# Attention of a LayerNorm, attention and low-rank FFN layer on 8 cores: K of the later half as a stage of its own, the quadratic in two VectorE operations, the output copies on VectorE

## The reference

```python
def polymax(x):                       # in place of softmax; x_int=-100, y_int=1
    lin  = where(-100 <= x <= 0, -0.01 * x + 1, 0)
    poly = where(x > 0, x ** 2 + 1, 0)
    return (poly + lin) / 1000
def attn(x, W_attn, W_proj):          # 16 heads of 64
    q, k, v = split(x @ W_attn)
    att = einsum('bhid,bhjd->bhij', q, k) / 8
    att = where(causal, att, -inf)
    return einsum('bhij,bhjd->bhid', polymax(att), v) @ W_proj
x = x + attn(layernorm(x), W_attn, W_proj)           # x: (4, 4096, 1024) f32
x = x + ffn(layernorm(x), U1, V1, b1, U2, V2, b2)    # rank 256, 4096 wide, gelu
```

## Time and profile before

| | us |
|---|---|
| median of 3 runs | 2106.52 (2102.57 to 2109.41) |
| the profiled execution, its own time | 2104.88 |
| its span on core 0, the slowest | 2103.3 |
| spans of the other cores | 2085.1 to 2102.9 |
| granted clock of TensorE, mean, core 0 | 0.732 of full speed |
| attention half 0, from its first scores to its last copy | 512.0 to 1189.1 |
| from there to the first matmul of V of the later half | 1189.1 to 1246.1 |
| running sums and V of the later half | 1246.1 to 1357.5 |
| attention half 1 | 1357.5 to 1620.8 |

### The profile page before, as it was taken

One profiled execution on the slowest core, in us unless ns is written; L12 is line 12 of the kernel. 1 busy time (PEld: TensorE's weight loads), 2 busy tenths in 40 slices (PEclk: granted clock), 3 DMA queues, 4 the chain that ended last, 5 costly groups with the idle time before them and its releaser, 6 DMA issues.

```text
span 2103.3 us, 22645 instructions; the slowest of 8 cores (2085.1 to 2103.3 us)
## 1 busy us (share of the span) xinstructions
PE 1285.4 (61%) x6801; PEld 457.9 (22%) x6880; DVE 1232.6 (59%) x2043; ACT 786.0 (37%) x1202; POOL 0.2 (0%) x4
## 2 busy tenths in 40 slices
PE   3423286477776676767667427666775461367786
PEld 0001132243222222212112113322221130023332
DVE  4558433244677887888878513489997233344422
ACT  1200000001667776767667400167776000133333
POOL 0000000000000000000000000000000000000000
PEclk8755597799566677777877769955666685579988
DMA  5545201200000000000000220000000444001111
GB/s 164 160 128 191 80 22 59 80 1 11 21 8 18 16 6 16 8 16 6 16 18 6 76 89 1 1 1 1 1 1 21 156 136 128 0 0 41 40 40 41
DMA packets 53335, 96.08 MB, mean 46 GB/s; under 512 B 2529, under 2 KB 24290, under 8 KB 53218
## 3 DMA queue, kind: packets, MB, share of 16 engines
q1 hardware_dynamic: 46498, 84.14, 12.6%
q10 hardware_dynamic: 6720, 10.49, 1.6%
HBM read 82.04 MB, written 12.58 MB: 45 GB/s over the span
## 4 chain that ended last, share of the span: by engine, by line
PE 44%; DVE 24%; issue 13%; DMA 11%; ACT 5%; SPq 1%; DVEq 1%; ACTq 0%
DVE poolD L766 12%; PE ps L801 7%; DMA poolD<-W_attn 6%; PE ps L732 5%; PE ps L851 4%; PE ps L1132 3%; PE ps L940 3%; PE ps L633 3%; PE ps L1038 3%; PE ps L655 3%; PE ps L613 3%; PE ps L1152 3%; ACT poolD L753 3%; DMA poolD<-W_proj 2%; DVE poolC L498 1%
## 5 line engine op out<-in xcount | busy, mean ns | idle before, releaser
L753 ACT ACTIVATE poolD<-ps 128x1024 bf16<-128x1024 f32 (+3 forms) x640 | 561.1, 907 | 739.9 <-PE ps L732 620.6
L766 DVE SCALAR_TENSOR_TENSOR poolD<-poolD 128x1024 bf16<-128x1024 bf16 (+3 forms) x640 | 654.5, 1062 | 69.3 <-ACT poolD L753 35.7
L801 PE MATMUL ps<-poolD,poolA 128*64 128x512 bf16 (+3 forms) x1280 | 299.2, 455 | 223.8 <-DVE poolD L766 114.9
L732 PE MATMUL ps<-poolB,poolA 64*128 64x512 bf16 (+3 forms) x1280 | 275.1, 456 | 56.5 <-ACT poolD L753 26.0
L801 PEld LDWEIGHTS ps<-poolD,poolA 128*64 128x64 bf16 x1280 | 89.1, 117 | 405.4 <-issue 403.7
L1144 ACT ACTIVATE poolC<-ps,sb_b1s 128x512 bf16<-128x512 f32 x128 | 87.6, 687 | 114.8 <-PE ps L1132 71.6
L758 ACT ACTIVATE poolD<-ps,consts 128x256 bf16<-128x256 f32 x256 | 124.3, 486 | 0.0
L732 PEld LDWEIGHTS ps<-poolB,poolA 64*128 64x128 bf16 x1280 | 64.4, 101 | 242.1 <-issue 241.7
L851 PE MATMUL ps<-poolC,poolD 128*128 128x512 bf16 x224 | 106.5, 476 | 0.0
L940 PE MATMUL ps<-poolD,poolC 128*128 128x512 bf16 x241 | 59.5, 393 | 58.8 <-DVE poolD L912 57.9
L809 PE MATMUL ps<-poolD,poolA 128*64 128x128 bf16 x512 | 83.0, 297 | 0.0
(11 more groups left out here) (100 smaller groups left out, 1135.2 us busy)
## 6 DMA issues: line engine op xcount, KB each, us to landing
poolD<-x_t SPq DMA_DIRECT2D x8, 2048.0 KB, 9.2
poolA<-x_t SPq DMA_DIRECT2D x8, 2048.0 KB, 9.6
poolD<-W_attn SPq DMA_DIRECT2D x12, 1024.0 KB, 4.9
poolD<-W_attn SPq DMA_DIRECT2D x16, 512.0 KB, 3.9
poolC<-x_own_t SPq DMA_DIRECT2D x8, 1024.0 KB, 5.8
y<-poolC SPq DMA_DIRECT2D x4, 2048.0 KB, 6.9
kf2scratch<-poolD SPq DMA_DIRECT2D x32, 128.0 KB, 1.7
poolA<-kf2scratch SPq DMA_DIRECT2D x4, 1024.0 KB, 15.6
```

The costliest lines, as they stand in the source:

```text
L732: e.matmul(o, l, r, skip_group_check=True, start=True, stop=True, tile_position=tp),
L753: e.activation(o, i, AF.Relu), inc="S")
L766: e.scalar_tensor_tensor(o, i, 0.01, i, ALU.add, ALU.mult),
L801: e.matmul(o, l, r, skip_group_check=True, start=st, stop=True, tile_position=tp),
```

## The change

Three things change. (1) With `K_ILV = False` all of the interleaved K work is gone from half 0: the 256 matmuls L851, the 32 copies L862 and their DMAs, the eight weight loads with L713, and the four DMAs that read the buffer back. In its place `p4_sweep(D, is_v=False)`, code that was there unused, runs between half 0 and the V sweep: it loads W of K in 8 pieces of 512 KB with their conversions, and then runs 32 groups of 8 matmuls of 512 columns, each copied by VectorE straight into kf; the 8 loads for V come after. (2) (r + 0.01) r is done as an addition of a constant into a new buffer ab2 (two slots) and then a product; the product waits for the addition, and the addition for the product two steps before. (3) The copies of the output at the end of a block are done by VectorE in half 0 too.

```diff
+        ab2 = [view(poolD, 14336, BF16, [128, 2, 512]),
+               view(poolD, 16384, BF16, [128, 2, 512])]
...
-            if half == 0:
+            if K_ILV and half == 0:
                 b.wait("sync", "T", p1_done["T"])
...
-                    if half == 0 and tb2 == 0:
+                    if K_ILV and half == 0 and tb2 == 0:
                         b.wait("sync", "V", kcast[hc - 1] if hc > 0 else p1_done["V"])
                         kdd = b.dma(kstage4[:, :, :],
...
                         b.wait("vector", "S", s_rel[sb])
+                        if idx >= 2:
+                            b.wait("vector", "V", gcnt[idx - 2])
+                        acnt = b.op("vector",
+                                    lambda e, o=ab2[idx % 2][:, :, 0:N],
+                                    i=eb[:, 2 * sb:2 * sb + 2, 0:N]:
+                                    e.tensor_scalar_add(o, i, 0.01), inc="V")
                         b.wait("vector", "T", g_rel[sb])
+                        b.wait("vector", "V", acnt)
                         gcnt[idx] = b.op("vector",
                                          lambda e, o=gb[:, 2 * sb:2 * sb + 2, 0:N],
+                                         a=ab2[idx % 2][:, :, 0:N],
                                          i=eb[:, 2 * sb:2 * sb + 2, 0:N]:
-                                         e.scalar_tensor_tensor(o, i, 0.01, i,
-                                                                ALU.add, ALU.mult),
-                                         inc="V")
+                                         e.tensor_mul(o, a, i), inc="V")
...
-                        if half == 0 and idx < 8:
+                        if K_ILV and half == 0 and idx < 8:
                             b.wait("tensor", "V", kcast[hc])
...
-                    if half == 0:
-                        b.wait("scalar", "T", tf_av)
-                    if half == 0:
+                    b.wait("vector", "T", tfence())
+                    if K_ILV and half == 0:
                         if ke_dma[kblk[0] % 2]:
...
-                        if half == 0:
-                            if chunk_final and j > 1:
-                                b.op("scalar", lambda e, o=dst, s=src,
-                                     pv=prefsnap[:, j, p:p + 1]:
-                                     e.activation(o, s, AF.Identity, bias=pv), inc="S")
-                            else:
-                                b.op("scalar", lambda e, o=dst, s=src:
-                                     e.mul(o, s, 1.0), inc="S")
-                        elif not chunk_final:
+                        if not chunk_final:
                             b.op("vector", lambda e, o=dst, s=src: e.tensor_copy(o, s),
                                  inc="V")
+                        elif c <= 1:
+                            if j == 1:
+                                b.op("vector", lambda e, o=dst, s=src: e.tensor_copy(o, s),
+                                     inc="V")
+                            else:
+                                b.op("vector", lambda e, o=dst, s=src,
+                                     pv=prefsnap[:, j, p:p + 1]:
+                                     e.tensor_scalar(o, s, pv, None, ALU.add), inc="V")
...
-        b.wait("sync", ke_dma[0], 16)
-        b.wait("sync", ke_dma[1], 16)
-        for i in range(4):
-            kfload.append(b.dma(kf[:, :, 512 * i:512 * (i + 1)],
-                                kf2_d[:, :, 512 * i:512 * (i + 1)]))
-        b.wait("vector", ke_dma[0], 16)
-        b.wait("vector", ke_dma[1], 16)
+        if K_ILV:
+            ...
+        else:
+            p4_sweep(D, is_v=False)
         p4_sweep(2 * D, is_v=True)
```

More of the change, by code:

```diff
@@ L231, in build_program @@
         abh = view(poolD, 13824, BF16, [128, 2, 128])
+        K_ILV = False
         kstage4 = view(poolD, 20480, F32, [128, 8, 128])
@@ L526, in emit_sweep_kt @@
                 b.wait("tensor", "V", sweep_state["snapV"])
-                if half == 1:
+                if K_ILV and half == 1:
                     b.wait("tensor", kfload[ktloc // 4], 16)
@@ L853, in emit_attention @@
                     av_done = b.cnt["T"]
-                    tf_av = tfence()
-                    b.wait("vector", "T", tf_av)
-                    if half == 0:
-                        b.wait("scalar", "T", tf_av)
-                    if half == 0:
+                    b.wait("vector", "T", tfence())
+                    if K_ILV and half == 0:
                         if ke_dma[kblk[0] % 2]:
@@ L950, in build_program @@
         b.wait_all("vector", h0_done, sems=("T", "S"))
-        b.wait("sync", ke_dma[0], 16)
-        b.wait("sync", ke_dma[1], 16)
-        for i in range(4):
-            kfload.append(b.dma(kf[:, :, 512 * i:512 * (i + 1)],
-                                kf2_d[:, :, 512 * i:512 * (i + 1)]))
-        b.wait("vector", ke_dma[0], 16)
-        b.wait("vector", ke_dma[1], 16)
+        if K_ILV:
+            b.wait("sync", ke_dma[0], 16)
+            b.wait("sync", ke_dma[1], 16)
+            for i in range(4):
+                kfload.append(b.dma(kf[:, :, 512 * i:512 * (i + 1)],
+                                    kf2_d[:, :, 512 * i:512 * (i + 1)]))
+            b.wait("vector", ke_dma[0], 16)
+            b.wait("vector", ke_dma[1], 16)
+        else:
+            p4_sweep(D, is_v=False)
         p4_sweep(2 * D, is_v=True)
```

## The result

The changed kernel takes 2131.6 us against 2108.4 before (medians of 8 runs each); the ratio is 1.0118, with a 95% interval of 1.0102 to 1.0134. It is slower by 1.2%, outside the range of 2068 to 2122 around the 2085 us of the forecast. In some executions one die shows a lower granted clock and takes longer; medians here are over all runs, ratios and their intervals leave those executions out.

The account below looks back on a forecast made before the run. VectorE bounds half 1; in half 0 K's TensorE work and weight DMA waits add to it. Half 0 -94.1, stretch to V +72.5, half 1 +1.4: -20.2 us on 2104.88, so 2085 us, range 2068 to 2122.

Parts of the forecast that it names:

- part 2: (r + 0.01) r as addition (0.424 us) and product (0.69 us), dependent gap 0.04 us; was to bring 11 us.
- the first rival: Dependent wait between addition and product costs 0.11 us instead of 0.04: +36 us, 2121 us; chance 8%.
- part 1: K moved from half 0 into its own stage: half 0 82.5 us less, stretch to first V matmul 72.5 more.
- the third rival: K nearly free in half 0, its own stage dearer; low clock stays, loads slower: 2100 to 2107 us; chance 10%.
- second rival: The addition runs at twice, not four times, the rate: 2222 us; chance 5%.
- Part 3: Half 0's output copies on VectorE cost nothing, covered by its wait for scores and relu; 36 us if uncovered.

Follow-up runs that it names:

- E2: Changed kernel with the product's wait for the addition attached to the product instead of an instruction of its own; 2091.8 us, ratio 0.9927.
- E13: Kernel before, with all waits directly ahead of a VectorE or ScalarE operation attached to it; 2082.6 us, ratio 0.9855.
- E15: Changed kernel, with all waits directly ahead of a VectorE or ScalarE operation attached to it; 2064.8 us, ratio 0.9772.
- E1: Changed kernel with (r + 0.01) r as one operation again, K stage and copies on VectorE kept; 2107.4 us, ratio 1.0003.
- E11: Kernel before, K still inside half 0, with the two operations and the product's wait attached; 2093.3 us, ratio 0.9929.
- E6: Changed kernel with the output copies of half 0 on ScalarE again; 2144.5 us, ratio 1.0150.
- E4: Changed kernel with the product taking r twice, so it does not wait for the addition (0.01 r left out of the result); 2031.2 us, ratio 0.9643.
- E3: Changed kernel with the next step's addition queued ahead of the product, three slots of ab2; 2163.6 us, ratio 1.0270.
- E8: E3 with two staging buffers in the three weight loads, first two V pieces fetched during K's matmuls; 2114.7 us, ratio 1.0004.

## Why the prediction was wrong

**The step that failed** is in part 2: "the dependent pair L451, L452 starts 0.72 us apart with a duration of 0.68, so duration + 0.04". The row was read rightly and stood for another thing: L452 carries its wait, while the product's is an instruction of its own in the queue. The code showed this, `ss=True` at L452 and `b.wait` in the diff. In the changed kernel the gap is 0.10 us, the value at which the prediction said that it would fall. That is the first rival, which had a chance of 8% and a price of 36 us. E2 undoes it by the form of the wait alone and lands at 2091.8 us, on a chip where the kernel before takes 2106.1: 14 us faster, with 20 forecast. With all waits attached on both sides it is 17.8 us (E13, E15).

**Why 2131 and not the rival's 2121.** The rival's 36 us are 25 in half 0 and 11 in half 1. E1 gives the base for it: there half 0 takes 598.2 us, and the split adds 11.8 where -12.9 was forecast, and in half 1 13.2 where 1.4 was, so it costs 25 and 12 us more than forecast. The rest is 2 us in half 0 from part 1, 1.6 us in the K stage, 2.1 in the V sweep and 7.5 in stages that were not touched; 3.2 of these are the profiled execution's own distance from the median. That the rival's price fits so well is in part luck: from the changed kernel to E2 the two halves gain 31 and 12 us, so the form costs 43 and not 36, and the forecast without it was 6 us too high in half 0, for the reason given under "the low clock" below.

**Part 1, K out of half 0**: both sizes held, half 0 598.2 us against 594.6 and 1.3 for the last copies, and the stretch 130 against 129.5. The gain of some 9 us that was their difference is gone: E1 finds +1 us with an interval of 5 us to each side, and E2 and E11 say the same with the faster pair. Half 0 of the kernel before was taken from core 0, where it is 677.1 us; the median of the cores is 674.7. From it, K outside saves 76.5 us in half 0 and costs 77.0 behind it. So the outcome that the third rival names, that K was nearly free in half 0 and its stage is the dearer one, is what came for this part. Its terms did not: in a long block of E1 the granted clock is 0.59 at first (881.8 to 888.6) and 0.82 behind, so it does not stay low, and the two loads took 36 to 37 us each, not 39.4.

The argument that TensorE holds back the first eight steps because of K explains little of half 0. It did not enter the sum. In the kernel before, VectorE stops once in a long block of the sort, for 0.36 us, and the block takes 962.61 - 941.04 = 21.57 us against 20.89 in E1; of the 76.5 us, 41.3 are the eight waits for the weights of K (last line: us in total, times, longest):

```profile
941.04 5.94 DVE L766 SCALAR_TENSOR_TENSOR poolD<-poolD 128x1024 bf16<-128x1024 bf16 x5 [1.03 <-ACT poolD L753]
947.34 12.58 DVE L766 SCALAR_TENSOR_TENSOR poolD<-poolD 128x1024 bf16<-128x1024 bf16 x11 [0.36 <-PE ps L801]
962.61 3.50 DVE L766 SCALAR_TENSOR_TENSOR poolD<-poolD 128x1024 bf16<-128x1024 bf16 x3 [1.03 <-ACT poolD L753]
```

```profile
DVE poolD L713 <- DMA poolD<-W_attn: 41.3, 8, 6.3
```

**Part 2, the rates**: 0.421 us for the addition against 0.424, 0.692 for the product. Both halvings do combine. The Trainium skill (VectorE: DVE Perf Modes, The perf-mode tier table) has this fourfold rate, and the trace agrees. The advice of the Trainium skill to minimize the number of operations and not semaphores (VectorE: DVE Perf Modes, Rules for kernel authors) is not borne out here. Two operations beat the one by 0.8% when the product carries its wait (E2 at 0.9927 against E1 at 1.0003) and lose 1.1% when it does not, so how the wait is given decides 40 us. The prediction tied that advice to its second rival, which is about the rate of the addition; the number of operations does not give that time.

**Part 2, the low clock**: a second term was wrong, and small. The forecast had "at low clock TensorE needs 0.54 + 0.57 = 1.11, so there only 0.03 us is gained". TensorE does need 1.11 us, but VectorE goes at 1.06 all through the block (E2). With 0.07 us in each of 16 steps a long block comes to 20.9 - 1.1 = 19.8 us, and 19.73 were measured, against 19.9. In half 0 the split gains 19.4 us from E1 to E2 where 12.9 were forecast. This error and the 9 us of part 1 go in opposite directions, so that the total came near the forecast in E2 is luck in part. Masked blocks of c = 0 take 12.21 us against 12.25.

**Part 3** cost nothing, as forecast, and E6 shows that it gains 0.3%, which was not: the relu no longer stands behind the copies.

**The second rival** (half the rate) did not occur, and the long blocks were put together rightly, 20.89 us in E1 against 20.8.

## What to carry to other kernels

Ahead of splitting an operation in two, take the gap between dependent neighbours from a pair whose wait is written in the same way; with 640 such pairs in 2100 us, 0.07 us decided the sign here. Take the size of a stage from the median of the cores, not from one. Let the operation that has to wait carry the wait itself. And an independent operation that is moved into a gap must not be the one that was filling another.

## What was not expected of the hardware

- A wait that is an instruction of its own adds 0.06 to 0.08 us to a hand-over that ends last: VectorE to itself 0.10 against 0.03 to 0.04 us, ScalarE and TensorE to VectorE 0.10 to 0.11 against 0.03 to 0.04. In the kernel before, which has no split, attaching them all is worth 1.5%.
- Independent neighbours on VectorE start 0.08 to 0.09 us before the end of the one before; a dependence costs that too. Without it the same instructions are worth another 60 us (E4 against E2).
- With the order of E3, which hides the dependence, half 0 takes 23 us more, and TensorE's granted clock in it is 0.53 instead of 0.69. Why is open.
- At a granted clock of 0.50 TensorE takes 1.11 us a step and VectorE still 1.06: an engine that is a little slower for a few steps need not hold up the next one (E2).
- With one staging buffer a 512 KB piece comes every 4.4 us, with two every 2.8 (E8).
